# Numbering destination windows from the last to the first in a graph network kernel, with the empty tiles in front

## The reference

```python
dst = minimum((6250 * uniform((200000,)) ** 2.0).astype(int32), 99999)   # sorted afterwards, src random
# layer 1, three times:   out = clip(segment_sum(norm[:, None] * out[row], col) * 0.9 + 0.1 * y, 0, 1)
# layer 2, six times:     msg = einsum('ei,eio->eo', out[src], w_e)      # w_e: a 32x32 matrix of each edge
#                         m = relu(segment_sum(msg, dst) + conv_bias);  out = h = gru_cell(m, h)
# layer 3, once:          relu(segment_sum(h[src], dst) * norm_dst @ weight + bias)
# layer 4, once:          segment_sum(ew * x[row], col), with self loops
x = layernorm(x + layer(x))
```

## Time and profile before

| | |
|---|---|
| median of 3 runs | 29634.66 us (29593.76 to 29645.51) |
| the profiled execution's own time | 29624.24 us |
| its span | 29622.5 us |
| mean granted TensorE clock | 0.694 of full speed |
| TensorE matmuls busy | 15680.3 us (53%) |
| GpSimd busy | 18912.0 us (64%) |
| VectorE busy | 8084.4 us (27%) |
| ScalarE busy | 5957.2 us (20%) |
| moved by DMA | 2428.17 MB, mean 82 GB/s |

### The profile page before, as it was taken

The page is one execution under the profiler, slowest core; times in us unless marked ns, Lnnn a source line. Parts: engine busy times, 40 slices in busy tenths (PEclk is TensorE's granted clock), DMA queues, the critical chain, the costliest instruction groups (busy, mean ns, idle before and its releaser), DMA issues. The chain is left out here.

```text
span 29622.5 us, 431499 instructions
## 1 busy us (share of the span) xinstructions
PE 15680.3 (53%) x96083; PEld 12493.8 (42%) x96083; DVE 8084.4 (27%) x16291; ACT 5957.2 (20%) x14071; POOL 18912.0 (64%) x20031
## 2 busy tenths in 40 slices
PE   3333841221221258867876886886787788112112
PEld 3333421121121246655655664665565567112112
DVE  5444521111111123323332332332333233101111
ACT  0000510000000023423433442342343344000000
POOL 4887047757757657737737746774773774675775
PEclk5555965555555578988887897897888789555555
DMA  3222622322322324534433443452443444222222
GB/s 99 49 49 49 219 79 46 51 40 47 51 39 47 49 75 113 128 77 107 125 89 100 121 117 78 114 128 74 110 126 86 103 122 106 40 48 46 42 48 43
DMA packets 5514647, 2428.17 MB, mean 82 GB/s; under 512 B 4822474, under 2 KB 5290186, under 8 KB 5392764
## 3 DMA queue, kind: packets, MB, share of 16 engines
q1 hardware_dynamic: 4404056, 1640.66, 22.4%
q0 software_dynamic: 650176, 469.34, 9.1%
q10 hardware_dynamic: 459168, 307.23, 3.3%
HBM read 1850.82 MB, written 557.33 MB: 81 GB/s over the span
## 5 line engine op out<-in xcount | busy, mean ns | idle before, releaser
L763 POOL DMA_INDIRECT sb_xg<-node_rows,sb_idx x9408 | 8927.8, 949 | 3157.0 <-issue 2669.3
L982 POOL DMA_INDIRECT sb_xg<-node_rows,sb_idx x7840 | 7408.0, 945 | 3516.3 <-issue 2387.0
L870 PE MATMUL banks<-sb_spread,sb_eh_sb 128*128 128x256 f32 x29184 | 8029.2, 437 | 2228.8 <-DMA sb_eh_sb<-eh 2226.1
L870 PEld LDWEIGHTS banks<-sb_spread,sb_eh_sb 128*128 128x128 f32 x29184 | 6288.2, 221 | 3674.0 <-issue 2113.2
L826 DVE TENSOR_TENSOR sb_spread<-sb_xs,banks_p 128x2048 f32<-128x2048 f32 x1824 | 4172.0, 2288 | 9161.5 <-PE banks L870 8892.0
L924 ACT ACTIVATE sb_g<-banks 128x512 f32<-128x512 f32 x7296 | 4357.2, 597 | 7152.2 <-PE banks L870 7027.5
L1074 PE MATMUL banks_s<-sb_mask,sb_xs 128*128 128x32 f32 x6080 | 1452.1, 403 | 7744.8 <-DMA sb_xs<-gathered_rows 7744.8
L1074 PEld LDWEIGHTS banks_s<-sb_mask,sb_xs 128*128 128x128 f32 x6080 | 1353.5, 328 | 7844.7 <-issue 7301.3
L1050 DVE COPY sb_s<-banks_s 32x32 f32<-32x32 f32 x3040 | 568.3, 187 | 8437.2 <-PE banks_s L1074 8292.2
L343 POOL DMA_INDIRECT slots<-sb_rows,sb_slot_u x1600 | 2106.2, 1316 | 774.5 <-issue 757.7
L1145 ACT ACTIVATE sb_stat<-sb_stat 98x64 f32<-98x64 f32 x4 | 1.0, 256 | 10853.0 <-DVEq L1137 10853.0
(11 more groups left out here) (212 smaller groups left out, 9388.4 us busy)
## 6 DMA issues: line engine op xcount, KB each, us to landing
sb_eh_sb<-eh SPq DMA_DIRECT2D x912, 1024.0 KB
sb_xs<-gathered_rows SPq DMA_DIRECT2D x26752, 16.0 KB
sb_xg<-node_rows,sb_idx POOLq DMA_INDIRECT x17248
eh<-sb_eh_sb ACTq DMA_DIRECT2D x304, 512.0 KB, 3.2
gathered_rows<-sb_xg POOLq DMA_DIRECT2D x588, 256.0 KB
gathered_rows<-sb_xg ACTq DMA_DIRECT2D x980, 128.0 KB, 1.7
sb_win_row<-window_rows SPq DMA_DIRECT2D x100, 488.3 KB
slots<-sb_zeros SPq DMA_DIRECT2D x19, 2368.0 KB
```

Of the source, the lines that this page charges most:

```text
L763: nc.gpsimd.indirect_dma_start(m.xg_two[h][:, t * D:(t + 1) * D], None, m.node_dram, bass.IndirectOffsetOnAxis(ap=m.idx_two[h][:, t:t + 1] ...
L870: o = mm(m.ps_pair[u % 4][:, v, :, :], m.eh[h % 2][:, t * K:(t + 1) * K], m.spread[t // TS][:, t % TS, :, :], start=True, stop=True)
L982: nc.gpsimd.indirect_dma_start(m.xg[h][:, t * D:(t + 1) * D], None, m.node_dram, bass.IndirectOffsetOnAxis(ap=m.idx[h][:, t:t + 1], axis=0 ...
```

## The change

Windows are numbered from the last to the first: the new number is 783 minus the old one. Tile numbers begin at `PAD` = 2432 - 1562 - 784 = 86, so the empty tiles are tiles 0 to 85; their row is 0. `win_of` turns the number back (`NW` - begun), which is 784 and no window for the empty tiles. The digits `whi` and `wlo` are made from the new number. Positions of edges, rows and the list of sources follow from it.

```diff
@@ -45,6 +45,7 @@
+PAD = TP - (EDGES - 1) // P - NW
@@ -157,7 +158,11 @@
-            for out, x, shift, mask in ((m.win, m.dst, 3, 0xffff), (m.whi, m.dst, 7, 0xffff), (m.wlo, m.dst, 3, 15),
+            do(V.tensor_scalar(m.tmp_i[:, :], m.dst[:, :], 3, 0xffff, ALU.logical_shift_right, ALU.bitwise_and))
+            do(V.tensor_scalar(m.win[:, :], m.tmp_i[:, :], -1.0, float(NW - 1), ALU.mult, ALU.add))
+            do(V.tensor_copy(m.key_i[:, :], m.win[:, :]))
+            do(V.tensor_scalar_add(m.win[:, :], m.win[:, :], float(PAD)))
+            for out, x, shift, mask in ((m.whi, m.key_i, 4, 0xffff), (m.wlo, m.key_i, 0, 15),
                                         (m.shi, m.src, 6, 0xffff), (m.slo, m.src, 0, 63)):
@@ -272,13 +277,14 @@
             tile_number(m.first, m.first_slot, 0)
+            do(V.tensor_scalar_add(m.first[:, :], m.first[:, :], float(PAD)))
             for c in range(OC):
                 do(V.tensor_scalar_add(m.tnum[:, :], m.pcol[:, :], float(OQ * c)))
                 do(V.tensor_scalar(b[0:OQ, :], m.first[0:OQ, :], m.tnum[0:OQ, 0:1], None, ALU.is_le))
                 do(V.tensor_reduce(m.begun[:, :], b[0:OQ, :], AX, ALU.add))
                 do(V.tensor_tensor(m.row_of[:, c:c + 1], m.tnum[0:OQ, :], m.begun[:, :], ALU.subtract))
-                do(V.tensor_scalar_add(m.win_of[:, c:c + 1], m.begun[:, :], -1.0))
-            do(V.tensor_scalar(m.row_of[:, :], m.row_of[:, :], 1.0, float(JT - 1), ALU.add, ALU.min))
+                do(V.tensor_scalar(m.win_of[:, c:c + 1], m.begun[:, :], -1.0, float(NW), ALU.mult, ALU.add))
+            do(V.tensor_scalar(m.row_of[:, :], m.row_of[:, :], float(1 - PAD), 0.0, ALU.add, ALU.max))
@@ -1497,7 +1503,7 @@
-                m.src, m.dst, m.tmp_i = (sb(n, [EQ, ET], I32) for n in ("src", "dst", "tmp_i"))
+                m.src, m.dst, m.tmp_i, m.key_i = (sb(n, [EQ, ET], I32) for n in ("src", "dst", "tmp_i", "key_i"))
```

## The result

The changed kernel takes 28333.86 us (median of 4 runs, 28330.04 to 28334.17), the kernel before, run beside it, 29634.32 us (4 runs, 29593.76 to 29645.51): a ratio of 0.9563, 95% interval 0.9547 to 0.958. The forecast was 28355 us. The profiled execution spans 28332.5 us, 1290.0 less than the one before, with a mean granted clock of 0.703 after 0.694.

The account below looks back on a forecast made before the run. GpSimd's gathers bound each pass early, SyncE's issue late. From 29624.2 us, minus 868 (convolutions) and 408 (plain), plus 2.6 (setup), came 28351; with runs' median 10 above the profiled execution, 28355 was given, range 28230 to 28460.

Parts of the forecast that it names:

- What bounds the kernel: Message passes: GpSimd's gathers produce without waiting; late in a convolution SyncE's issue limits, 12.88 us a batch, not TensorE.
- The arithmetic of the order: Old tile order: SyncE follows GpSimd until row 1023, tile 1359; 67 batches remain, fetches end at 2268 us in a convolution.
- Convolution, step by step: Convolution tail: GpSimd is last, then three batches follow; sum begins at 2169.6 us, saving 144.7 a pass, 868 for six.
- Plain: Plain passes: from GpSimd's end through loads and fold to the sum, 1988.5 against 2070.1 us; saves 81.6, 408 for five.
- Added work: VectorE's setup: three more operations, serial and uncovered, add 2.6 us.
- The clock: Convolution tail, TensorE: by the skill three batches each 2 us longer, 36 in all; by rows only halves after a wait.
- (a): Convolutions: SyncE stays the bound, deciding from 13.8 us a batch; 28585 us at 14.0; chance 0.06 at moderate cost.
- (b): All passes: shared transfers slow GpSimd's gathers; slower kernel from 5.7% dearer, 29920 us at 7%; chance 0.04, 0.02 slower.
- (c): Convolution tail longer than stepped through: one chunk more late costs 128 us over six passes, 28480 us; chance 0.10.
- (d): Whole change has no effect: waits for each half batch's last row keep the lag, 29627 us; chance 0.02.
- what was to be seen in the trace: Gaps from GpSimd's last store to sum 71 and 28 us; early stretches 23 batches in 300 us, last ones 14.

Follow-up runs that it names:

- e4: Kernel before, with a 17th row transfer that nobody reads per convolution batch in SyncE's queue: 29222.21 us, ratio 0.9872.
- e9: Kernel before, with one more semaphore increment per convolution batch in SyncE's code and no added transfer: 29203.1 us, ratio 0.9862.
- e3: Changed kernel, with a 17th row transfer that nobody reads per convolution batch in SyncE's queue: 28286.77 us, ratio 0.9556.
- e10: Changed kernel, with GpSimd's index copy issued in the chunk before and a 17th SyncE transfer per convolution batch: 27914.32 us, ratio 0.9427.
- e5: Changed kernel, with six more row transfers that nobody reads per convolution batch in SyncE's queue (22 instead of 16): 29839.31 us, ratio 1.0077.
- e6: Changed kernel, with GpSimd's copy of a chunk's indices issued in the middle of the chunk before: 27910.44 us, ratio 0.9426.
- e1: Kernel before, with only the window order reversed and the empty tiles left at the end: 28997.55 us, ratio 0.9796.
- e2: Kernel before, with only the 86 empty tiles put in front and windows in the old order: 28887.11 us, ratio 0.9759.
- e8: Changed kernel, with index copy ahead and SyncE's weight load before the next batch's row transfers, on a slow chip: 46886.43 us, ratio 0.9876.
- e12: Changed kernel, with index copy ahead and SyncE's weight load before the next batch's row transfers, on another chip: 27832.56 us, ratio 0.9404.

## Why the prediction was right

**What bounds the kernel** held in its frame and in one content not. That GpSimd produces without waiting, that the first part of a pass is its, that the late part is SyncE's: a faster SyncE gains 380 to 408 us in the kernel before (e4, e9) and nothing in the changed one (e3, e10), a much slower one costs (e5), and a faster GpSimd counts in full (e6). "It is SyncE's issue that limits, not TensorE" was right on TensorE and half right on the rest: of 12.88 us a batch, 11.2 are issue and 1.7 are a stall at the loop's jump. The two rows that stood there, 12142.56 and 12194.09, were four batches apart, and the division by four hid it. It did no harm to the forecast, because the mean rate is what the kernel before runs at, and because in the changed kernel the rate falls out altogether. It did harm to the forecast of e4: there the price of one transfer was added to a rate of which a part could vanish.

**The arithmetic of the order** (crossing at r = 1023, 2268 against 2268.4) is borne out by its consequences. (From its own numbers 1.34/0.805 = 1.66 the crossing comes out nearer r = 1030; the end moves by 1 us.) With the measured rates in its place it gives e4's passes within 4 us, e9's within 7 to 14 and e5's first within 11, and e1 and e2 came within 72 and 33 us of what was worked out from it.

**Convolution, step by step.** The last store ends 2100.6 us after the pass's start (2099.1 said); the load of batch 149's weights is issued 9.0 us later (9.4 said), 5.1 to the matmul (5.0), 10.9 for that batch (11.3), 2.4 to the next (2.4), 10.9 (10.9), 1.1 to the third (2.4), 9.2 for it (9.9), and 18.5 from 12448.55 to the sum (19.1). Together 2167.8 against 2169.6, saved 146.5 against 144.7. What misses are the terms of the third batch, which came back to back, and not one of the steps is missing or too many. Part of the closeness is luck: the tail behind the last store is 67.2 us where 70.5 were said, and GpSimd's side is 1.5 longer. SyncE's waits for landed rows in this pass are where they were said to be: between 10360 and 11880 it has none, from 11880 to 12400 it has 18, of 128.9 us, and one of 22.8 for the last two chunks.

**Plain.** 1988.5 against 1988.5, and this exactness is luck: two terms miss in opposite senses, GpSimd's side with 1963.2 instead of 1960.0 and what lies behind it with 25.3 instead of 28.5. The other four plain passes take 1986.5 to 1987.4.

**Added work.** The first pass starts 5.6 us later, where 2.6 were said; but in e3, which has the same added work, it starts 4.4 us earlier than in the kernel before, so these starts don't measure it. Nothing on the scale of the result.

**The clock.** The prediction took from the rows that only the halves after a wait are slow, and from the Trainium skill's rule that the last three batches would each run some 2 us longer. Of the six halves in the tail, two take 5.42 and 5.39 us and the others 3.70 to 3.72. The first follows the wait of 21.84 us, in which the granted clock fell to a mean of 0.54, and is 1.7 us longer; there the Trainium skill's rule ("TensorE: Matmul & The Clock Gate", section "HAM oscillation — how this bites in real kernels") agrees. The other batches follow no such wait, and the rule was stretched in being applied to all three. Nor is the rows' reading quite right: the half of 5.39 us follows no transfer, in the tail as in the earlier trace rows (12789.04), where it stood in the 10.9 us of its batch. So the sum was unharmed. The granted clock in the starved stretch is 0.78, in the busy one 0.91.

**The rivals.** (a) SyncE as the bound from 13.8 us a batch on: there is a threshold (e5), and the changed kernel lies under it; in the first convolution its batches take 12.6 to 13.3 us from the third turn of the loop until the waits begin. (b) Gathers slowed by the shared transfers: the mean of a gather is 951 ns where it was 949, but 948 in e3 with the same order, and GpSimd has 253 records in 300 us everywhere. (c) A chunk more late: the tail has no such step. (d) No effect: excluded by each half of the change. TensorE's clock as the cause: in e9 SyncE's queue alone was edited, TensorE's work stayed as it was, and the time moved by 408 us. Of what was to be seen in the trace, the gaps behind GpSimd are 67 and 25 us where 71 and 28 were said, and one number is off: 12000 to 12300 holds 16.3 batches (1241 / 76), and even the last 300 us before GpSimd's last store hold 15.1 (1146 / 76), not 14; no term of the sum hung on it.

## What to carry to other kernels

When one engine fills a table and another drains it, the order of the work is free time: let the items that need little of the producer come first and the dense ones last, so that the consumer has nothing saved up when the producer ends. The gain is what lies behind the producer's end, it can be read as one difference of two rows for each pass, and it is capped there; after that only the producer's own rate counts (0.72 us a chunk were worth some 400 us), and the consumer's rate doesn't matter up to a threshold that can be worked out (11.65 and 12.9 us a batch gave the same time, 15.47 gave 1500 us more). Before a period is divided by the number of items in it, look at each gap: one in four may be something else.

## What the runs showed of the hardware

- The gap at the jump back of a loop on SyncE's queue is 8.0 us in the kernel before and 1.72 us once one increment of a semaphore is added to its body four times over, with 1158 instruction packets against 108. Directly behind the branch it is 5.35 us against 0.24. In the kernel before this was worth 408 us, 1.4%. In the changed kernel one transfer more for each batch ends it too, six more leave it (1164 packets), and with SyncE's steps swapped 2.41 us are left behind the branch (1159 packets).
- An added instruction can so make a queue faster: e3 and e4 issue 912 transfers more than the kernels they start from, and SyncE's batch got some 1.2 us shorter.
- Row transfers stand 0.52 us apart in SyncE's queue within a half batch (8 in 3.97 us, the last one of 0.33) and 0.48 where six more stand in a row (2.76 us). The 0.56 of the mean over a batch's 16 (9.0 us) holds the load of the second half's row numbers.
- One chip ran the same kernel in 47473 us instead of 29600, with SyncE's queue slow in stretches (25.2 us a batch in the mean) and the computing engines as fast as elsewhere: a time from another chip means nothing without the kernel before beside it, and even the ratio does not carry over, since another engine sets the time there (the same kernel has 0.9876 there as e8 and 0.9404 elsewhere as e12).
